# Attention queries in items of eight heads, with most projections inside unrolled attention steps

## The reference

```
h = layernorm(x)
qkv = h @ Wqkv                     # 32 query heads of 16, one key and one value head
scores = q k^T / 4 + slope_h * (pos_k - pos_q), causal
x = x + softmax(scores) v @ Wo
h = layernorm(x)
x = x + h @ W_base^T + b + lora of the two best of eight experts
```

## Time and profile before

| | |
|---|---|
| median of 3 runs | 771.75 us (771.06 to 771.91) |
| profiled execution | 768.09 us, span 766.0 us |
| PE busy | 688.5 us (90%) |
| DVE busy | 575.9 us (75%) |
| ACT, POOL busy | 356.9 us (47%), 187.7 us (25%) |
| moved by DMA | 56.06 MB, 73 GB/s on the mean |

### The profile page before, as it was taken

The page is one execution under the profiler, slowest core; times in us unless marked ns, Lnnn a source line. Parts: engine busy times, 40 slices in busy tenths (PEclk is TensorE's granted clock), DMA queues, the critical chain, the costliest instruction groups (busy, mean ns, idle before and its releaser), DMA issues.

```text
span 766.0 us, 16023 instructions
## 1 busy us (share of the span) xinstructions
PE 688.5 (90%) x4224; PEld 298.8 (39%) x4224; DVE 575.9 (75%) x1851; ACT 356.9 (47%) x493; POOL 187.7 (25%) x340
## 2 busy tenths in 40 slices
PE   4495636989999999999999999999999999999997
PEld 2242312333343343343344343343343345555553
DVE  5375434999988988988988988988987156666664
ACT  2133110245665766666776666666665821111111
POOL 0010101132242242242242142242243132222221
PEclk9889777999999999999999999999999999999999
DMA  9559698111033034034034136910000029910001
GB/s 240 91 145 133 116 130 235 57 38 68 33 52 65 31 44 69 31 43 70 33 48 68 39 59 91 119 38 15 31 15 15 32 89 165 188 46 36 28 27 55
DMA packets 37592, 56.06 MB, mean 73 GB/s; under 512 B 6028, under 2 KB 19468, under 8 KB 37524
## 3 DMA queue, kind: packets, MB, share of 16 engines
q1 hardware_dynamic: 33164, 44.98, 33.6%
q0 software_dynamic: 1792, 6.29, 2.4%
q10 hardware_dynamic: 2592, 4.26, 1.6%
HBM read 35.72 MB, written 19.79 MB: 72 GB/s over the span
## 4 chain that ended last, share of the span: by engine, by line
PE 72%; DMA 11%; DVE 11%; issue 4%; ACT 1%; SPq 0%; DVEq 0%; POOL 0%; POOLq 0%; ACTq 0%
PE psum L601 19%; PE psum L556 17%; PE psum L583 10%; PE psum L625 7%; PE psum L647 6%; PE psum L580 4%; DMA q_dram<-work 4%; DMA arena<-q_dram 4%; DMA x_sb<-in_x 3%; DVE psum L970 3%; PE psum L517 2%; DVE negm L975 2%; PE psum L642 2%; PE psum L657 2%; DVE negm L970 1%
## 5 line engine op out<-in xcount | busy, mean ns | idle before, releaser
L786 ACT ACTIVATE work<-psum 128x1024 f32<-128x1024 f32 (+1 forms) x320 | 289.7, 943 | 161.1 <-PE psum L583 136.2
L970 DVE CUSTOM_DVE_ANT_0 psum<-psum,future 128x384 f32<-128x384 f32 (+3 forms) x512 | 240.0, 517 | 31.6 <-PE psum L556 24.7
L556 PE MATMUL psum<-k_op,arena 106*128 106x512 bf16 (+3 forms) x768 | 209.6, 331 | 34.6 <-DMA arena<-q_dram 19.5
L975 DVE TENSOR_REDUCE negm<-psum 128x1 f32<-128x512 f32 x256 | 163.1, 684 | 28.4 <-PE psum L556 27.7
L601 PE MATMUL psum<-work,v_op 128*32 128x512 f32 (+3 forms) x1536 | 164.4, 500 | 0.4 <-POOL work L1155 0.4
L583 PE MATMUL psum<-arena,k_op 109*128 (+4 forms) x640 | 158.6, 316 | 1.0 <-ACT work L786 0.8
L1155 POOL TENSOR_SCALAR_AFFINE_SELECT work<-work 128x512 f32<-128x512 f32 x128 | 81.6, 637 | 276.0 <-ACT work L786 276.0
L556 PEld LDWEIGHTS psum<-k_op,arena 106*128 (+1 forms) x768 | 69.9, 97 | 191.7 <-issue 97.1
L517 PE MATMUL psum<-work,wqkv_sb 128*128 128x512 f32 (+1 forms) x160 | 83.2, 643 | 14.6 <-issue 13.9
L580 PE MATMUL psum<-arena,k_op 116*128 (+1 forms) x512 | 85.1, 221 | 0.0
L583 PEld LDWEIGHTS psum<-arena,k_op 109*128 109x128 bf16 x640 | 60.3, 98 | 35.7 <-ACT work L786 8.9
(11 more groups left out here) (84 smaller groups left out, 441.3 us busy)
## 6 DMA issues: line engine op xcount, KB each, us to landing
o_dram<-o_sb SPq DMA_DIRECT2D x32, 256.0 KB
q_dram<-work POOLq DMA_DIRECT2D x16, 384.0 KB, 3.1
arena<-q_dram SPq DMA_DIRECT2D x12, 512.0 KB, 17.3
arena<-q_dram SPq DMA_DIRECT2D x48, 128.0 KB, 5.5
arena<-o_dram SPq DMA_DIRECT2D x32, 128.0 KB, 8.7
arena<-rcp_dram SPq DMA_DIRECT2D x32, 128.0 KB, 9.2
out<-wqkv_sb ACTq DMA_DIRECT2D x16, 256.0 KB, 2.1
x_sb<-in_x SPq DMA_DIRECT2D x3, 1024.0 KB, 9.5
```

The costliest lines, as they stand in the source:

```text
L556: last = nc.tensor.matmul(bank[:, a * width:(a + 1) * width], q_op[0:ROW_MAX, bass.ds(col, P)], k_op[0:ROW_MAX, b, k0:k0 + width], start=T ...
L786: nc.scalar.activation(probs[:, n % 4, heads * hp:heads * (hp + 1), 0:w], src, ACT.Exp).then_inc(exp_done, 1)
L970: last = nc.vector.tensor_tensor_reduce(keys, keys, future[:, CH - width:CH], -1.0, 3e38, ALU.add, ALU.min, negm[:, late, 0, j * QT + t:j ...
L975: nc.vector.tensor_reduce(dst, psum[:, idx % NSB, 0:len(js) * width].rearrange("p (a k) -> p a k", a=len(js)), AX_X, ALU.max, negate=True) ...
```

## The change

**Order of the front.** Before step 0 PE turns chunk 0, does query item (0, 0) and the keys of chunk 0, turns chunk 1, does its values of chunk 0, item (1, 0) and the keys of chunk 1 (`BEFORE`). The rest stands in `AMONG`: six items, one set of values and the tiles of chunk 2 in step 0, everything else in steps 1 to 8. In these, projections are done in halves of 256 tokens.

**Banks.** In step 0 a side use takes banks 3 to 7 in turn; from step 1 on it is an element of the ring of three, among the slots (`places`). `pe_order` weighs side pieces in, and lets at most two slots stand between the four matmuls of a half.

**Queries.** SP loads each item (one chunk, one pair) by itself when it is stored, six DMAs of 128 KB. The constant rows of `q_op` are loaded pair by pair. DVE no longer waits for them before it splits; it splits the first two items, GpSimd the other fourteen, of which eight stand in steps at places in `SPLIT_AT`. ACT copies the values. `xnT`, `q4` and `qpart` lie in the arena and no longer in the buffer of probabilities.

**Loops.** All attention steps are written out on all engines. The FFN is as before.

```
+BEFORE = tiles_turned(0) + [("q", 0, 0, None), ("kv", 0, None, None)] + tiles_turned(1) + [
+    ("v", 0, None, None), ("q", 1, 0, None), ("kv", 1, None, None)]
+AMONG = {
+    0: [("v", 1, None, None)] + [("q", c, m, None) for m in (1, 2, 3) for c in (0, 1)] + tiles_turned(2),
+    1: halves("kv", 2),
+    2: [("v", 2, None, None)] + tiles_turned(3) + halves("q", 2, 0),
+    3: halves("kv", 3) + halves("q", 3, 0),
+    4: [("v", 3, None, None)] + halves("q", 2, 1) + halves("q", 3, 1),
+    5: halves("q", 2, 2),
+    6: halves("q", 3, 2),
+    7: halves("q", 2, 3),
+    8: halves("q", 3, 3),
+}
...
+        if piece[0] == "side" and piece[2]:
+            if k:
+                upto = max(put, min(upto, put + NSB - 1 - inside))
...
+    for u in range(N_FIRST):
+        use_at[u] = (NSB + u % (8 - NSB), ("side", u - (8 - NSB)) if u >= 8 - NSB else None)
+    for k, order in enumerate(ORDER):
+        for what, a, b in order:
+            if what == "slot" or (what == "side" and a >= N_FIRST and b == 0):
+                bank = e % NSB
+                e += 1
...
+SPLIT_AT = {(3, 0): 8, (4, 0): 9, (4, 1): 10, (5, 0): 11, (5, 1): 12, (6, 1): 13, (7, 1): 14, (8, 1): 15}
...
+            def load_queries(n):
+                c, g = Q_ITEMS[n]
+                sp.wait_ge(q_stored, 16 * (n + 1))
+                if n >= 2:
+                    sp.wait_ge(q_in[n % 2], 96 * (n // 2))
+                if c >= 2:
+                    sp.wait_ge(s_full, NSC * 2 * (g + 1))
+                for r, (a, _) in enumerate(PARTS):
+                    sp.dma_start(q_op_pairs[DH * r:DH * (r + 1), c % 2, g].rearrange("d (h q) -> d h q", q=CH),
+                                 q_dram[c, a, g * P:(g + 1) * P].rearrange("(h d) q -> d h q", d=DH)).then_inc(q_in[n % 2], 16)
...
+            load_x(2)
+            load_x(3)
             load_queries(0)
             load_queries(1)
-
+            load_constants(1)
+            step(0)
+            load_queries(2)
+            load_queries(3)
+            step(1)
...
+            def max_slot(k, r):
...
+                if s == 0 and r in (0, EARLY_SLOTS):
+                    pe.wait_ge(q_in[1 if r else 0], 96 * (PAIRS * b + g + 1))
...
+            def query_hi(u, c, m, half):
...
+                if not half:
+                    if 2 <= n < 4:
+                        act.wait_ge(q_split_v, n - 1)
+                    elif n >= 4:
+                        act.wait_ge(q_split_p, n - 3)
+                nc.scalar.mul(q4[:, n % 2, columns], psum[:, USE_AT[u][0], 0:CH if half is None else CH // 2], QSCALE
+                              ).then_inc(side_free, 1)
+                if half == 0:
+                    return
...
-            dve.wait_ge(c_in, 16 * N_C)
-            among = early_slots()
...
+            split_queries(0)
             dve.wait_ge(w_in, 16 * N_W)
+            for piece in range(KEY_PIECES):
+                split_keys(0, piece)
+            statistics(2)
+            split_queries(1)
+            dve.wait_ge(c_in, 16 * N_C)
...
+            def split_queries(n):
+                pool.wait_ge(q_hi_ready, n + 1)
+                nc.gpsimd.tensor_tensor(out=q4[:, n % 2], in0=q4[:, n % 2], in1=qpart[:, n % 4, 0], op=ALU.subtract).then_inc(q_chain, 1)
...
+                store_queries(n)
```

More of the change, by code:

```diff
@@ L132, in pe_order @@
             break
+    side = list(AMONG.get(k, ()))
+    whole, extra = sum(w for w, _ in work), sum(sum(use_parts(use)) for use in side)
+    merged, done, beside = [], 0, 0
+    for w, piece in work + [(0, None)]:
+        while side and (piece is None or (beside + sum(use_parts(side[0])) / 2) * whole <= done * extra):
+            merged += [(v, ("side", USES.index(side[0]), part)) for part, v in enumerate(use_parts(side[0]))]
+            beside += sum(use_parts(side.pop(0)))
+        if piece is not None:
+            merged.append((w, piece))
+            done += w
     slots = [("slot", k, r) for r in range(NSL)] if k < NK else []
-    total = sum(w for w, _ in work)
-    out, done, put = [], 0, 0
-    for w, piece in work:
+    total = whole + extra
+    out, done, put, inside = [], 0, 0, 0
+    for w, piece in merged:
         done += w
         upto = min(NSL - 1, round(NSL * done / (SLOTS_BY * total)))
+        if piece[0] == "side" and piece[2]:
+            if k:
+                upto = max(put, min(upto, put + NSB - 1 - inside))
+            inside += len(slots[put:upto])
+        else:
+            inside = 0
         out += slots[put:upto]
@@ L468, in _ @@
             load_heads(1)
-            with sp.Fori(0, PAIRS - 2) as i:
-                step(NB + 4, i)
-                step(NB + 5, i)
-            step(NK)
-            step(NK + 1)
+            for k in range(NB + 4, NK + 2):
+                step(k)
             sp.wait_ge(pv_done, NTI * NK)
@@ L603, in values_product, with step @@
                 last.then_inc(pv_done, 1)
-            def step(k, i=None):
-                for what, m, n in pe_order(k):
-                    if k == 1 and what == "scores" and n == (0, 1):
-                        values(NCH - 1)
+            def step(k):
+                for what, m, n in ORDER[k]:
                     if k == NK and what == "scores" and n in OUT_AMONG:
@@ L786, in exps @@
                     nc.scalar.activation(probs[:, n % 4, heads * hp:heads * (hp + 1), 0:w], src, ACT.Exp).then_inc(exp_done, 1)
+                    for u in behind.get((n, hp), ()):
+                        side(u)
                     if hp == 0 and n == LAG - 1 and m:
@@ L801, in step @@
                 m = k - 1
+                behind = uses_behind(k)
+                for u in behind.get(None, ()):
+                    side(u)
                 for n in range(NTI):
-                    exps(m, n, i)
+                    exps(m, n, i, behind)
+                    if k == 1 and n == 3:
+                        rstd_first(3)
                     if k == NK and n == 5:
@@ new lines, in _ @@
+            for r in range(NSL):
+                step(1, None, (r,))
+                if r == 4:
+                    statistics(3)
+                if r == 16:
+                    normalised(3, (0, 1))
+                if r == 20:
+                    normalised(3, (2, 3))
+            for k in (2, 3, 4):
+                for r in range(NSL):
+                    step(k, None, (r,))
+                    if k % 2 == 0 and r % 4 == 3 and r // 4 < KEY_PIECES:
+                        split_keys(k // 2 + 1, r // 4)
@@ L1022, in _ @@
+            for k in range(5, NK):
+                step(k)
+                if k == NB + 2:
                     reciprocals(0)
[L1023 to L1026 removed]
             def residual(n, i):
```

477 lines of the change are left out of this document (237 added, 240 removed).

## The result

The changed kernel takes **747.67 us** (746.60 to 749.28, four runs) against 771.40 of the kernel before measured beside it: a ratio of 0.9694, with a 95% interval of 0.9671 to 0.9717. It is faster, by 24 us and not by the forecast 48; 747.67 lies just above the upper end of the range, 746. The profiled execution took 748.7 us, its span 746.9, so the median lies 0.8 us above this span.

What follows compares the result with a forecast made beforehand. Front bound by round trips through memory and early loads, steps by PE with DVE close behind. Span 766.0 - 81.7 - 8.0 + 37.2 + 10.8 - 8 + 2 = 718.3; with 2.1 and 3.7 added, 724 us; range 702 to 746.

Steps and rivals of the forecast that it cites:

- When step 0 starts: Front: first query item projected, split, stored and loaded back by 38 us, bounds 34 and 50.
- Step 0: First attention step, with six query items in it: 36 us long, so step 1 starts at 74, gaining 81.7 us.
- Unrolling: Attention steps written out instead of looped: 28.01 us each instead of 28.71, 8.0 us gained over fourteen intervals.
- Side work: Steps 1 to 8: moved projections, tiles and values, bank waits, filled waits and DVE's extra work, 42.0 us given back together.
- item 5: Steps 1 to 8: slots wait for ACT to copy a half projection's bank, 18 times 0.6 us, +10.8; bounds 0 and 29.
- Item 6: Steps 1 to 8: added PE work shrinks the mutual waiting of PE and DVE, -8 us; bounds 0 and 20.
- The step that failed: Fourteen of sixteen query splits on GpSimd, 4 to 5 us an item, costed at nothing because GpSimd has idle time.
- The rival that named GpSimd: Steps: ACT waits for GpSimd's split and all exponentials with it, 776 us, slower than before; chance 0.03.
- Nothing: Later steps: loads of single query items, x2, weights and constants cost no time.
- The last terms: Added to the span of 718.3: 2.1 us around it and 3.7 to the median of the runs.
- the ring costs twice: Steps: bank waits cost twice the estimate, or unrolled PE code is fetched late, 750 us; chance 0.09.
- steps 5 to 8 over 34: Sign of a wrong forecast: these steps lasting over 34 us, not 31 to 32, would fault item 5.

Runs made afterwards that it cites:

- e3: The changed kernel with GpSimd's splits of query items 2 to 7 (step 0) done on only 8 of 512 columns: 746.19 us.
- e7: e1 with one more query projection, the third item, put ahead of step 0's first slot: 721.61 us.
- e6: The kernel before the change with only its looped attention steps written out: 758.53 us.
- e1: The changed kernel with GpSimd's splits of query items 10 and 12 to 15 moved from the end of a step to its middle: 726.16 us.
- e10: e1 with the splits of query items 8 to 15 done on DVE between slots, their stores left on GpSimd: 736.73 us.
- e11: e10 with GpSimd's store of query item 10 moved to the end of step 4: 728.25 us.
- e5: e1 with the projections of steps 1 to 8 at full width (512 columns) instead of in two halves: 737.09 us.

## Why the prediction was right and wrong

Right in direction, and twice too large in size: 48 us forecast, 24 measured. By its own items:

1. *When step 0 starts*: 38 forecast, 37.61 measured, in part by luck. The split ended at 22.33 and not 24.0; the store took until 29.6, 7.0 us by the chain and not 4; the load then lasted 7.9, where I had 7.1 and 3 for the x ahead of it. No row shows this term of 3 us for 1 MB.
2. *Step 0*: 36 forecast, 43.1 in this profile, 39.6 to 39.9 in others of the same step. Missing were 1.5 us and some 1.2 for DVE operations that GpSimd blocked twice, and 2.1 where the clock falls a second time. After the wait for the first load the first projection pairs take 1.92 instead of 1.02, which stands in e3's 38.15, too, and which e7 removes. PE also stood 1.46 us for ACT's copy of the last tile.
3. *Unrolling*: 8.0 forecast, 11.3 in the same intervals by e6. In the changed kernel a plain step is 27.61.
4. to 7. *Side work*: 42.0 forecast. In e1 the fourteen intervals are 436.8, fourteen plain ones and the reciprocals' 1.4 are 387.9, so 48.9. An interval with one query item is 4.54 above a plain one: 3.44 of PE, two waits of 0.48, and 0.1. The bank's wait (item 5) was well estimated: 17 times 0.5 us, 8.1, against 18 times 0.6, 10.8. Item 6, the filling of mutual waits, was wrong. The 12.7 us of the earlier trace rows are waits of weight loads (PEld), which overlap with running matmuls; PE's own waits for DVE in the same 56 us of the kernel before were these:

```profile
PE psum L556 <- DVE negm L970: 0.4, 2, 0.2
PE psum L556 <- DVE negm L975: 0.3, 2, 0.2
```

In e1 the weight loads' waits for DVE are 7.5 us in a plain step and 4.9 in one with a query item: they did shrink, and no time came of it. Without side work the fourteen intervals were forecast 5.9 us too long (393.8 against 387.9), and the side work 6.9 too short; that the sum is right to a microsecond, 436.8 against 435.8, is luck.
8. ***The step that failed.*** "Costed at nothing: in step 0 six items are at most 28 us of 36, and in the steps it is idle 39 us of 56." It measured 21.3 us in the intervals, 21.5 by the medians (e1), and in step 0 1.5 to 2.7 us of collisions with DVE (e3, e10). The length of a split was right; the cover was judged by GpSimd's mean idle time, while what counts is the idle time at the place in its order where the split stands. Five of eight splits stand at a step's end, where eight tiles in a row need a select: the last four of the late half and the first four of the next step. I wrote that if the cover goes, "every exponential waits behind it" through ACT. The trace lists no wait of ACT for GpSimd: the chain is GpSimd's select, PE's values product, and then PE's clock. The rival that named GpSimd had the engine right and the waiting one wrong; its 0.03 was for a case worse than this.
9. *Nothing* for the loads: in e1 intervals 6 and 7 last 32.14 and 32.15 at DMA shares of 0.44 and 0.34, which agrees.

The last terms, 2.1 + 3.7 us from the span to the median, were 0.8 here, so the forecast held 5.0 too many; by spans alone the miss is 28.6: 6.7 up to the first score, 22.3 in the intervals, less 0.4 by which the sum's marks (155.7 and 401.8) differ from those used here (155.87 and 402.02). The rule of the Trainium skill (GPSIMD Engine Reference, Engine selection) that elementwise work belongs on VectorE I had set against 14 us for the splits of steps 2 to 8 left on DVE; these eight cost 2.1 us there (e11), far less than the changed kernel's places on GpSimd and a little more than good ones.

The rivals: "the ring costs twice" gave 750, near the measured time, but by a mechanism that e1 and e5 exclude. Among the signs I had set, "steps 5 to 8 over 34" came true, and I had tied it to item 5; e1 shows that it was item 8.

## What to carry to other kernels

An in-order engine that is 30% busy is free only at some places. Before work is put on it, write down what follows that work in its order, who waits for that, and how long the gap at this very place is; five splits moved by four tiles were worth 21 us, ten times the choice between the engines. And a wait of PE can cost more than its length: here waits of 2.5 us cost 2.6 to 5.2, so count up to twice until a profile shows that the clock holds. Last, waits of weight loads for an engine are no time of PE until PE's own waits say so.

## What was unexpected of the hardware

- DVE's scalar_tensor_tensor of 96x512 takes 0.74 us alone and 1.6 when a GpSimd operation on SBUF of 1.15 us has started 0.1 us before, while GpSimd's stays at 1.15: DVE waits for nearly the whole of it. Two normalisations of 128x512 take 2.1 to 2.3 us instead of 1.0 when a split on GpSimd starts inside them.
- A program whose attention steps are all written out ran them at 27.6 to 27.7 us, two unrolled ones between looped ones at 28.0, looped ones at 28.7.
- The same step 0 is 39.6 to 39.9, 41.0 or 43.1 us long in different executions, by whether a second such collision comes about and whether the clock falls behind waits of 1.0 and 1.7 us.
